# A Mamba block and a mixture of experts on one core: front stages further ahead, another order in each slot, all four scans in PSUM

## The chip, the cores and the metric

The kernel runs on one core of one Trainium2 chip. The metric is the device time of one execution in microseconds, as the median of several runs. All data are fp32.

## The reference

The input x has 8 sequences of 1024 tokens with 256 features. Cut to what matters:

```python
x = x + mamba(layernorm(x))            # mamba itself returns its input plus its output
x = x + moe(layernorm(x))

# mamba: d_inner 512, 16 states, conv of 4 taps, dt_rank 16
u, z = split(norm(x) @ W_in.T)
u = silu(causal_conv(u) + conv_b)
dt, B, C = split(u @ W_xp.T);  dt = softplus(dt @ W_dt.T + b_dt)
for t:  h = exp(dt[t] * A) * h + dt[t] * u[t] * B[t];  y[t] = sum_n(h * C[t])
out = (y + u * D) * silu(z) @ W_out.T

# moe: 8 experts, each token goes to its best 2
logits = x @ router_w + router_b;  w = softmax(top2(logits))
out[token] = sum over its two experts of w * (silu(x @ gate_e) * (x @ up_e)) @ down_e
```

## The kernel before, in words

The tokens are cut into 16 chunks q of 512 tokens, two to a sequence. The scan of a chunk is cut into 16 units (u = 16 q + n): unit n holds 4 of the 16 states for 128 of the 512 inner channels, spread as 4 tiles j of 128 partitions by 512 time steps. Two chunks make a group of 1024 tokens, whose MoE runs as 23 tiles of 128 sorted rows, each with the weights of one expert (768 KB, loaded anew for each tile).

Every engine runs the same loop over slots s (one scan unit each, then the slots of the tail), and in each slot its own part of several stages, in an order written out by hand. The engines are tied together by semaphores alone, and each executes its own instructions in order. A slot therefore has no fixed time; an engine can be a slot or two ahead of another as far as its waits allow.

- **The scan.** GpSimd (POOL) makes dt·u·B for the four tiles (`drive`, line 979, two instructions of 128x1024, one slot ahead, into one of three buffers `hs`). ScalarE (ACT) makes exp(dt·A) into the PSUM tile `dA` (`decay`, line 697). VectorE (DVE) scans tiles 0 and 1 in place in `dA` and multiplies both with C (`unit_first`, lines 778 and 789). In `unit_last` it scans tile 3 into `hs` in SBUF, then tile 2 in place, and multiplies tile 2 with C (line 800). GpSimd multiplies tile 3 with C (`weigh`, line 990). TensorE (PE) sums over the states into `yps` (its `weigh`, line 523).
- **The front and tail stages of a chunk** go through one PSUM bank `ring`, one item after the other: PE fills it, ACT (for O: DVE) empties it. The items are X0, X1 (transposes of the normalised input), U0 to U3 (projection to u), W0 to W3 (conv), P0 (projection to dt, B, C), D0 to D3 (dt projection, with the softplus after D1 and D3), Z0 to Z3 (projection to z), and for the chunk before O0, O1 (output projection), F0, F1 (transposes), R0 (router) and, for the second chunk of a group, K0 (ranks). `FRONT_RING` and `TAIL_RING` give the slot n of each. PE and ACT take the first item of a slot, then part of the MoE work, then the second item, then the rest.
- **Softplus.** ACT computes exp, 1+e and ln in `softplus`; DVE computes a rounding term (`round_off`, line 804); GpSimd adds it and multiplies with u (`dtu`, lines 996 to 1001, in slots 11 and 15). SP stores dt and dt·u to DRAM (`store_dt`, line 329) and loads them back spread over the partitions (`load_rep`, line 341).
- **Routing.** `route` (slot 5) adds the router bias on DVE (827), takes the top two and builds one-hot rows (827 to 841). `place` (slot 6) computes where each row goes, `scatter` (slots 7 to 14, GpSimd's indirect DMAs) sorts the rows into DRAM, `gather` (8 slots in a row after the last tile) brings two result rows per token back, and `combine` (one slot later, line 895) adds them.
- **MoE tiles.** Tile k passes through the slots at = k (transpose, line 542, eviction 712), k+1 (gate and up, 553, tanh 718), k+2 (`activate`, 885 and 888), k+3 (down, 534) and k+4 (store). SP's `load_tile` loads the sorted rows `xt` (353) and the gate and up weights (356) of tile at+1, after `store_tile` and `load_down` of the slot.

All plain DMAs are issued by SP, in one queue, in order; a wait on SP holds back every load behind it.

## Time and profile before

| | |
|---|---|
| median of 3 runs | 3042.28 us (3037.51 to 3044.11) |
| the profiled execution, its own time | 3046.68 us |
| its span in the profile | 3044.9 us |
| TensorE clock granted, mean | 0.817 of full |

The profile shows one execution. Its busy time per engine is a sum over stages that have different limits; the span runs from the first instruction to the last. Line numbers are those of the kernel before. In the rows a group of instructions is named line, engine, operation, output<-input; "idle before" is the idle time of that engine ahead of the group, and what ended it.

### The profile page before, as it was taken

The page shows a single profiled execution, that of the slowest core. Times are in us where ns is not written, and L with a number is a line of the kernel's source. Part 1 is how long each engine was busy: PE and PEld are TensorE (multiplying, and loading weights), DVE is VectorE, ACT ScalarE, POOL GpSimd, SP SyncE. Part 2 cuts the span into 40 slices and gives each one's busy share as a digit, 9 for nine tenths or more (in the row PEclk, how much of TensorE's full clock was granted, in tenths as well). Part 3 has the DMA queues.
Part 4 walks back from the last instruction along what each step waited for, and adds up shares of the span by engine and source line. Part 5 has one row for each costly group of instructions (what it writes and reads, how often), then busy time and mean ns, then how long its engine had stood idle before and what let it go on. Part 6 is the DMA issues. An engine that isn't in the chain of part 4 may idle for free.

```text
span 3044.9 us, 34043 instructions
## 1 busy us (share of the span) xinstructions
PE 1986.4 (65%) x8672; PEld 1105.0 (36%) x8672; DVE 2249.9 (74%) x3168; ACT 1533.8 (50%) x2414; POOL 2113.2 (69%) x1499
## 2 busy tenths in 40 slices
PE   4465665786747685586846867487764868556564
PEld 1112131444315351254414443154522535144453
DVE  0498988887868688787877878687887878789322
ACT  2565746465544655456454565446544564534111
POOL 0697869767696678867697676967688666976312
PEclk9687877798868897798867988688977989668888
DMA  3533343667457764566637574567736766375576
GB/s 122 141 91 96 95 114 84 179 169 187 110 158 184 183 185 113 163 185 177 159 112 197 155 202 116 149 177 189 190 99 169 191 163 173 110 200 158 163 213 193
DMA packets 271490, 473.01 MB, mean 155 GB/s; under 512 B 36928, under 2 KB 114752, under 8 KB 271168
## 3 DMA queue, kind: packets, MB, share of 16 engines
q1 hardware_dynamic: 259008, 437.26, 53.6%
q0 software_dynamic: 12288, 33.57, 3.5%
q8 instruction: 72, 1.18, 0.2%
q14 instruction: 122, 1.00, 0.1%
HBM read 372.38 MB, written 98.30 MB: 155 GB/s over the span
## 4 chain that ended last, share of the span: by engine, by line
POOL 32%; issue 17%; DVE 15%; PE 14%; DMA 9%; SPq 6%; ACT 6%; POOLq 0%; DVEq 0%; ACTq 0%
POOL hs L979 16%; DMA xt<-sorted_x 6%; DVE dA L778 5%; POOL sorted_x L1007 4%; PE p_g L553 4%; DVE hs L778 3%; POOL hs L990 3%; POOL pair L1017 2%; POOL dtb L998 2%; POOL dtub L996 2%; PE ring L443 2%; PE ring L435 2%; SPq L341 2%; DMA out<-xr 1%; PE p_a L534 1%
## 5 line engine op out<-in xcount | busy, mean ns | idle before, releaser
L979 POOL TENSOR_TENSOR hs<-rep_dtu,b_bc 128x1024 f32<-128x1024 f32 x512 | 1195.8, 2360 | 24.1 <-DMA rep_dtu<-dt_d 14.3
L697 ACT ACTIVATE dA<-rep_dt,a_s 128x512 f32<-128x512 f32 x1024 | 675.8, 684 | 616.3 <-DVE hs L789 453.7
L523 PE MATMUL yps<-hs,const_s 128*32 128x512 f32 x2048 | 335.0, 730 | 361.6 <-POOL hs L990 327.0
L990 POOL TENSOR_TENSOR hs<-hs,c_bc 128x512 f32<-128x512 f32 x256 | 330.5, 1291 | 343.9 <-DVE hs L778 333.0
L778 DVE TENSOR_TENSOR_SCAN dA<-dA,hs 128x512 f32<-128x512 f32 x384 | 453.5, 1211 | 56.1 <-POOL hs L979 46.7
L778 DVE TENSOR_TENSOR_SCAN dA<-dA,carry,hs 128x512 f32<-128x512 f32 x384 | 476.6, 1272 | 14.8 <-POOL hs L979 11.7
L553 PE MATMUL p_g<-xy,w_e 128*128 128x128 f32 x2944 | 424.1, 306 | 41.5 <-DVE hT L888 41.4
L553 PEld LDWEIGHTS p_g<-xy,w_e 128*128 128x128 f32 x2944 | 414.7, 223 | 75.2 <-issue 72.3
L435 PE MATMUL ring<-xnT,w_in_s 128*128 128x512 f32 x512 | 329.8, 778 | 104.3 <-ACT sz L634 64.3
L789 DVE TENSOR_TENSOR hs<-dA,c_bc 128x1024 f32<-128x1024 f32 x256 | 312.1, 1219 | 4.4
L885 DVE SCALAR_TENSOR_TENSOR th<-th,p_g 128x256 f32<-128x256 f32 x184 | 76.5, 416 | 312.1 <-ACT th L718 312.0
L712 ACT ACTIVATE xy<-p_a 128x512 f32<-128x512 f32 (+1 forms) x208 | 113.3, 545 | 326.4 <-PE p_a L542 298.2
L443 PE MATMUL ring<-ubuf,d_conv 128*128 128x512 f32 x512 | 249.1, 631 | 4.7 <-ACT ubuf L625 3.3
L542 PE MATMUL p_a<-const_s,xt 128*128 128x128 f32 x368 | 87.4, 325 | 246.1 <-DMA xt<-sorted_x 220.9
L895 DVE SCALAR_TENSOR_TENSOR xr<-pair,w,xr 128x256 f32<-128x256 f32 x64 | 73.7, 1151 | 219.2 <-DMA pair<-sorted_y,pos 210.1
L523 PEld LDWEIGHTS yps<-hs,const_s 128*32 128x32 f32 x2048 | 46.2, 117 | 513.9 <-issue 458.7
L1017 POOL DMA_INDIRECT pair<-sorted_y,pos x128 | 125.1, 977 | 152.7 <-DMA sorted_y<-xy 90.7
L435 PEld LDWEIGHTS ring<-xnT,w_in_s 128*128 128x128 f32 x512 | 109.7, 238 | 283.9 <-issue 143.1
L534 PE MATMUL p_a<-w_e,hT 128*128 128x256 f32 x736 | 209.7, 411 | 1.1 <-DVE hT L888 1.1
L800 DVE TENSOR_TENSOR hs<-dA,c_bc 128x512 f32<-128x512 f32 x256 | 175.6, 686 | 4.4
L534 PEld LDWEIGHTS p_a<-w_e,hT 128*128 128x128 f32 x736 | 142.1, 204 | 70.1 <-issue 49.0
L1007 POOL DMA_INDIRECT sorted_x<-xf,pos x128 | 129.3, 1010 | 52.7 <-issue 50.8
(113 smaller groups left out, 2805.1 us busy)
## 6 DMA issues: line engine op xcount, KB each, us to landing
w_e<-in_w_moe SPq DMA_DIRECT2D x184, 512.0 KB
rep_dt<-dt_d SPq DMA_DIRECT2D x256, 256.0 KB
rep_dtu<-dt_d SPq DMA_DIRECT2D x256, 256.0 KB, 8.7
w_e<-in_w_moe SPq DMA_DIRECT2D x184, 256.0 KB
xt<-sorted_x SPq DMA_DIRECT2D x184, 128.0 KB
sorted_y<-xy SPq DMA_DIRECT2D x184, 128.0 KB
dt_d<-dtb SPq DMA_DIRECT2D x32, 512.0 KB
dt_d<-dtub SPq DMA_DIRECT2D x32, 512.0 KB
```

The costliest lines, as they stand in the source:

```text
L435: last = pe.matmul(ring[:], w_in_s[:, c, ch * P:(ch + 1) * P], xnT[:, c, :], start=c == 0, stop=c == DC - 1)
L443: last = pe.matmul(ring[:], d_conv[:, c, k, :], ubuf[:, c % 2, k:k + T], start=k == 0, stop=k == TAPS - 1)
L523: last = pe.matmul(yps[32 * j:32 * j + 32, :], sumsel, hs[:, u % 3, j, :], start=False, stop=g == G - 1, skip_group_check=True)
L534: last = pe.matmul(p_a[:, DM:2 * DM], hT[:, v % 2, c, :], w_e[:, v % 2, col:col + DM], start=c == 0, stop=c == DC - 1)
L553: last = pe.matmul(p_g[:, f, :], w_e[:, v % 2, col:col + P], xtT(v)[:, c, :], start=c == 0, stop=c == DC - 1)
L697: act.activation(dA[:, j, :], rep_dt[:, c % 2, j, :], ACT.Exp, scale=a_s[:, n, j:j + 1]).then_inc(s_exp, 1)
L778: return dve.tensor_tensor_scan(out_ap, dA[:, j, :], hs[:, u % 3, j, :], init, ALU.mult, ALU.add)
L789: dve.tensor_tensor(hs[:, u % 3, 0:2], dA[:, 0:2], c_bc[:, g, :].unsqueeze(1).to_broadcast([P, 2, T]), ALU.mult).then_inc(s_m01, 1)
L979: pool.tensor_tensor(hs[:, u % 3, a:a + 2], rep_dtu[:, c % 2, a:a + 2], b_bc[:, g, :].unsqueeze(1).to_broadcast([P, 2, T]), ALU.mult).then ...
L990: pool.tensor_tensor(hs[:, u % 3, 3], hs[:, u % 3, 3], c_bc[:, g, :], ALU.mult).then_inc(s_hp, 1)
L1007: pool.indirect_dma_start(out=sorted_x[g.b], out_offset=bass.IndirectOffsetOnAxis(ap=pos[:, g.b, k, i:i + 1], axis=0), in_=xf[:, (g.first ...
L1017: pool.indirect_dma_start(out=pair[:, v % 2, k, :], out_offset=None, in_=sorted_y[g.b], in_offset=bass.IndirectOffsetOnAxis(ap=pos[:, g.b, ...
```

## The change

- `FIRST` moves from -19 to -23, and every front item of a chunk is placed by its distance to the chunk's first unit (`PLACES`): X0, X1, U0 at -19, three slots earlier than before, P0 at -10 (before: -7), D0 and D1 at -9 (-6), D2 and D3 at -5 (-2), Z2 and Z3 at -4. O, F and R keep their slots, K0 comes one slot later.
- In each slot PE now does its `weigh`, then the MoE tile (down, transpose, gate and up), and then all ring items. ACT does two decays, `take_pa`, `tanh`, the other two decays, and then all ring items. DVE does `round_off`, `route`, `place`, `weights` and `combine` between `unit_first` and `unit_last`, where they came after `unit_last`.
- GpSimd's work on dt is split: `smooth` (two instructions) in slots 8 and 12, `dtu` (one) in slots 9 and 13. Its `weigh` is gone.
- All four scans write in place to `dA`; DVE multiplies tiles 2 and 3 with C in one instruction of 128x1024.
- SP: the sorted rows of tile at+1 are loaded first in a slot, before everything else, and its gate and up weights last. `store_dt` is in slots 10 and 14, `store_bc` in 7.
- The router's bias is added by one more matmul on PE; the one-hot rows are made by one DVE instruction in place of a copy and eight comparisons.
- Scatter starts one slot later; for all groups but the last the gathers are two slots apart; `combine` follows two slots after its gather.

```diff
-FIRST = -UN - 3
-SCATTER = 7
+FIRST = -UN - 7
+SCATTER = 8
...
-        self.gather = self.start + STAGES + 1
+        step = 2 if per == 1 else 1
+        self.gather = {k: self.start + STAGES + 1 + step * k for k in range(NT)}
...
-FRONT_RING = {0: ["X0", "X1", "U0"], 3: ["W0"], 4: ["U1"], 5: ["W1"], 6: ["U2", "U3"], 7: ["W2"], 8: ["W3"], 9: ["P0"],
-              10: ["D0", "D1"], 11: ["Z0", "Z1"], 12: ["Z2"], 13: ["Z3"], 14: ["D2", "D3"]}
-TAIL_RING = {1: ["O0"], 2: ["O1"], 4: ["F0", "F1"], 5: ["R0"], 6: ["K0"]}
+PLACES = {-19: ["X0", "X1", "U0"], -18: ["U1"], -17: ["W0"], -16: ["W1"], -13: ["U2", "U3"], -12: ["W2"], -11: ["W3"],
+          -10: ["P0"], -9: ["D0", "D1"], -8: ["Z0"], -6: ["Z1"], -5: ["D2", "D3"], -4: ["Z2", "Z3"],
+          17: ["O0"], 18: ["O1"], 20: ["F0", "F1"], 21: ["R0"], 23: ["K0"]}
+SMOOTH = {8: 0, 12: 1}
...
SP:
-            for s in range(-UN, TOTAL_SLOTS):
+            for s in range(FIRST, TOTAL_SLOTS):
                 q, n = s // UN, s % UN
                 front = 0 <= q + 1 < NQ
+                for g, at in moe_at(s):
+                    if 0 <= at + 1 < NK:
+                        load_tile(g, at + 1)
+                    if 0 <= at - 4 < NK:
+                        store_tile(g, at - 4)
+                for g, i in gathered(s - 3):
+                    store_out(g, i)
+                for g, i in gathered(s - 1):
+                    load_xr(g, i)
...
                 for g, at in moe_at(s):
-                    if 0 <= at - 4 < NK:
-                        store_tile(g, at - 4)
                     if 0 <= at - 1 < NK:
                         load_down(g, at - 1)
                     if 0 <= at + 1 < NK:
-                        load_tile(g, at + 1)
+                        load_expert(g, at + 1)
...
PE:
-                items = ring_in(s)
-                for item in items[:1]:
-                    through_ring(item)
                 for g, at in moe_at(s):
                     if 0 <= at - 3 < NK:
                         down(g, at - 3)
                     if 0 <= at < NK:
                         tile_transpose(g, at)
-                for item in items[1:2]:
-                    through_ring(item)
-                for g, at in moe_at(s):
                     if 0 <= at - 1 < NK:
                         gate_up(g, at - 1)
-                for item in items[2:]:
+                for item in ring_in(s):
                     through_ring(item)
...
ACT:
                 if scan:
-                    for j in (0, 1, 3):
+                    for j in (0, 1):
                         decay(s + 1, j)
...
                 for g, at in moe_at(s):
                     if 0 <= at < STAGES:
                         take_pa(g, at)
-                if scan:
-                    decay(s + 1, 2)
-                for item in items[1:2]:
-                    through_ring(item)
-                for g, at in moe_at(s):
                     if 0 <= at - 1 < NK:
                         tanh(g, at - 1)
-                for item in items[2:]:
+                if scan:
+                    for j in (2, 3):
+                        decay(s + 1, j)
+                for item in ring_in(s):
                     through_ring(item)
-                if n == 15 and 0 <= q + 2 < NQ:
+                if n == 12 and 0 <= q + 2 < NQ:
                     norm_x(q + 2)
...
DVE:
-                scan(u, 3).then_inc(s_h3, 1)
-                scan(u, 2).then_inc(s_scan, 1)
+                scan(u, 2)
+                scan(u, 3).then_inc(s_scan, 1)
                 dve.wait_ge(s_scan, 2 * u + 2)
                 if q % 2 == 0:
-                    dve.tensor_copy(carry[:, n, 2:3], dA[:, 2, T - 1:T]).then_inc(s_carry, 1)
-                dve.tensor_tensor(hs[:, u % 3, 2], dA[:, 2], c_bc[:, g, :], ALU.mult).then_inc(s_m2, 1)
+                    dve.tensor_copy(carry[:, n, 2:4], dA[:, 2:4, T - 1]).then_inc(s_carry, 1)
+                dve.tensor_tensor(hs[:, u % 3, 2:4], dA[:, 2:4], c_bc[:, g, :].unsqueeze(1).to_broadcast([P, 2, T]),
+                                  ALU.mult).then_inc(s_m2, 1)
...
+                if n in SMOOTH and 0 <= q + 1 < NQ:
+                    round_off(2 * (q + 1) + SMOOTH[n])
+                if tail and n == 6:
+                    route(q - 1)
...
POOL:
-                if 0 <= s < UN * NQ:
-                    weigh(s)
-                if n in (11, 15) and 0 <= q + 1 < NQ:
-                    dtu(q + 1, int(n == 15))
+                if n in SMOOTH and 0 <= q + 1 < NQ:
+                    smooth(q + 1, SMOOTH[n])
+                if n - 1 in SMOOTH and 0 <= q + 1 < NQ:
+                    dtu(q + 1, SMOOTH[n - 1])
```

## Rows read from the trace of the kernel before

**Rows 1.** Windows: us, PE, PEld, DVE, ACT, POOL busy, clock, DMA share, GB/s.

```profile
114.90:377.70 262.80, 160.37 (x500) 53.16 (x504) 235.09 (x286) 165.27 (x242) 232.56 (x152) 0.80 0.44 104
377.70:711.00 333.30, 228.26 (x932) 117.71 (x924) 268.27 (x365) 185.02 (x286) 247.54 (x170) 0.79 0.53 141
...
1424.60:1782.30 357.70, 245.90 (x1088) 139.56 (x1084) 280.68 (x397) 190.47 (x300) 263.76 (x186) 0.81 0.60 162
...
2497.10:2822.00 324.90, 210.69 (x996) 125.00 (x988) 279.84 (x378) 148.47 (x241) 245.68 (x159) 0.80 0.59 160
2822.00:3044.90 222.90, 119.28 (x748) 102.83 (x748) 51.95 (x145) 34.44 (x75) 48.17 (x53) 0.82 0.63 190
```

**Rows 2.** Windows: about slots 9 to 16 of the period from 1424.6.

```profile
1516.10:1618.60 102.50, 52.51 (x143) 16.70 (x141) 72.07 (x92) 58.92 (x82) 93.98 (x76) 0.65 0.42 120
```

**Rows 3.** Groups by form, whole run: busy us, mean ns | idle before.

```profile
L990 POOL TENSOR_TENSOR hs<-hs,c_bc 128x512 f32<-128x512 f32 x256 | 330.5, 1291 | 343.9 <-DVE hs L778 333.0
L789 DVE TENSOR_TENSOR hs<-dA,c_bc 128x1024 f32<-128x1024 f32 x256 | 312.1, 1219 | 4.4
L800 DVE TENSOR_TENSOR hs<-dA,c_bc 128x512 f32<-128x512 f32 x256 | 175.6, 686 | 4.4
L778 DVE TENSOR_TENSOR_SCAN dA<-dA,carry,hs 128x512 f32<-128x512 f32 x384 | 476.6, 1272 | 14.8 <-POOL hs L979 11.7 <-ACT dA L697 3.0
L778 DVE TENSOR_TENSOR_SCAN hs<-dA,carry,hs 128x512 f32<-128x512 f32 x128 | 163.3, 1276 | 0.0
L443 PE MATMUL ring<-ubuf,d_conv 128*128 128x512 f32 x512 | 249.1, 631 | 4.7 <-ACT ubuf L625 3.3 <-ACT uc L629 0.8 <-ACT lgr L680 0.6
```

**Rows 4.** Waits of the period 1424.6 to 1782.3: total us, times, longest.

```profile
DVE th L885 <- ACT th L718: 34.5, 11, 11.3
...
DVE xr L895 <- DMA pair<-sorted_y,pos: 28.3, 6, 9.3
PE p_a L542 <- DMA xt<-sorted_x: 28.0, 5, 9.7
```

**Rows 5.** Waits of SP's queue, whole run.

```profile
SPq L329 <- POOL dtub L1001: 328.5, 28, 28.4
```

**Rows 6.** Timeline of SP, 1748 to 1762: start us, us.

```profile
1749.93 0.35 SPq L356 DMA_DIRECT2D w_e<-in_w_moe  x1
...
1759.47 0.43 SPq L353 DMA_DIRECT2D xt<-sorted_x  x1
```

**Rows 7.** Timeline of PE behind it.

```profile
1767.30 0.69 PE L542 MATMUL p_a<-const_s,xt 128*128 128x128 f32 x2 [9.70 <-DMA xt<-sorted_x]
```

**Rows 8.** Timeline of DVE in `route`.

```profile
1485.07 0.75 DVE L827 TENSOR_TENSOR lg<-lgr,rb_s 128x32 f32<-128x32 f32 x1 [1.29 <-ACT lgr L680]
...
1486.26 1.84 DVE L832 TENSOR_TENSOR gap<-mx 128x4 f32<-128x4 f32 x1
...
1488.90 1.16 DVE L839 TENSOR_SCALAR hot<-const_s,ixf 128x8 f32<-128x8 f32 x8
1490.09 0.19 DVE L841 TENSOR_TENSOR hot<-hot 128x32 f32<-128x32 f32 x1
```

**Rows 9.** Timeline of POOL beside it.

```profile
1483.42 4.65 POOL L979 TENSOR_TENSOR hs<-rep_dtu,b_bc 128x1024 f32<-128x1024 f32 x2
```

**Rows 10.** Timeline of ACT, dt and softplus of one half chunk.

```profile
1772.12 1.06 ACT L653 ACTIVATE ubuf<-xn_t 128x1024 f32<-128x1024 f32 x1
1773.19 1.28 ACT L655 ACT_TABLE_LOAD   x1
```

**Rows 11.** Timeline of ACT around the first decays.

```profile
114.13 2.52 ACT L697 ACTIVATE dA<-rep_dt,a_s 128x512 f32<-128x512 f32 x4
116.59 2.06 ACT L597 ACTIVATE xn_t<-xs,rst 128x256 f32<-128x256 f32 x4
```

**Rows 12.** Windows of the last group's tiles, with and without gathers beside them.

```profile
2884.00:2925.00 41.00, 19.26 (x96) 16.77 (x97) 9.12 (x20) 4.47 (x10) 14.02 (x16) 0.70 0.64 192
2925.00:3008.00 83.00, 58.98 (x389) 50.41 (x387) 16.60 (x39) 17.07 (x36) 0.46 (x1) 0.94 0.79 238
```

More of the change, by code:

```diff
@@ L727, in _ @@
                     norm_x2(q - 1)
-                items = ring_in(s)
-                for item in items[:1]:
-                    through_ring(item)
                 for g, at in moe_at(s):
@@ L907, in _ @@
                         activate(g, at - 2)
+                if n in SMOOTH and 0 <= q + 1 < NQ:
+                    round_off(2 * (q + 1) + SMOOTH[n])
+                if tail and n == 6:
+                    route(q - 1)
+                for g in ALL:
+                    if s == g.scatter[0]:
+                        place(g)
+                    if s == g.scatter[0] + 1:
+                        weights(g)
+                for g, i in gathered(s - 2):
+                    combine(g, i)
                 if unit:
                     unit_last(s)
-                if n in (11, 15) and 0 <= q + 1 < NQ:
-                    round_off(2 * (q + 1) + (n == 15))
                 if unit and n in (4, 8, 12):
@@ L919, in _ @@
                     moments(1, q - 1)
-                if tail and n == 5:
-                    route(q - 1)
-                for g in ALL:
-                    if s == g.scatter[0] - 1:
-                        place(g)
-                    if s == g.scatter[0] + 1:
-                        weights(g)
-                if n == 13 and 0 <= q + 2 < NQ:
+                if n == 10 and 0 <= q + 2 < NQ:
                     moments(0, q + 2)
-                for g, i in gathered(s - 1):
-                    combine(g, i)
         @block.gpsimd
```

83 lines of the change are left out of this document (27 added, 56 removed).

## The prediction

> **What bounds the kernel now.** I read first the windows between the first scans of the chunks. They show a steady pattern: the first scan at 114.9 us, a first group of two chunks without MoE in 262.8 us, one of 333.3, then five periods of 32 slots like that from 1424.6, which takes 357.7 us, a last one of 324.9, and 222.9 us after the last scan [rows 1]. In the steady period DVE is busy 280.7 us and so idle 77; POOL is busy 263.8, PE 245.9, ACT 190.5. No engine is full. Each slot ends when DVE has scanned, so what counts is DVE's work plus the time in which DVE stands still.
>
> The idle time comes from three places. In slots 9 to 16 POOL is busy 94.0 of 102.5 us and DVE only 72.1: scatter, the three dt instructions and its own C product meet on POOL [rows 2]. This is 30 of the 77 us. Second, the waits of the period name what came late: `activate` waits 34.5 us for the tanh, which waits for PE, and PE's tile transpose waits 28.0 us for the sorted rows, `combine` 28.3 us for the gathered pair [rows 4]. Third, what is behind the late rows is SP: it stands 328.5 us in all before `store_dt` for POOL's last dt instruction, up to 28 us at once [rows 5]. The example at 1750: SP issues the expert weights of one tile at 1749.93, then reloads dt, B and C, and only at 1759.47 the sorted rows of the next tile [rows 6]. PE stands 9.7 us and gets them at 1767.30 [rows 7].
>
> **DVE's work after.** The second C product grows from 128x512 to 128x1024, from 686 to 1219 ns, so by 0.53 us in each unit [rows 3]: 17.1 us in a period of 32, 136 in all. No scan is added; the fourth moves its output from SBUF to PSUM, 1276 against 1272 ns [rows 3], which I take as nothing. In `route` the bias add (0.75 us), the copy and the eight comparisons (1.16 us) fall away [rows 8], and one comparison comes. It reads two SBUF tensors, and such an instruction is bounded by two rows: 0.19 us for the sum of the one-hot rows, 1.84 us for a 4-element subtraction that starts while POOL runs `drive` and ends at 1488.10, just when POOL does, at 1488.07 [rows 8, 9]. So `route` gains between 0.2 and 1.9 us; I take 1.5, because with its C product gone POOL is freer: 3 us a period. DVE's work in the steady period is 280.7 + 17.1 - 3 = 294.8 us.
>
> **POOL's work after.** 1.29 us per unit and a small copy go [rows 3], 41 us a period and more. Better, POOL no longer waits for DVE's third scan inside its slot; `drive` is held only by the three `hs` buffers, so POOL can be up to two slots ahead. In slots 9 to 16 its work falls from 94 to about 81 us, its dt work is in two pieces, and three to four of the gathers come there instead of all eight. DVE's own 72 us [rows 2] grow there by 8 times 0.53 and some waiting. POOL should no longer set these slots; I count that idle time as gone, but for what the dt chain itself costs (below). If POOL still set them, up to 9 us a period would come back (81 against 72).
>
> **SP.** The sorted rows are issued right behind the weights of the tile before: in the example at about 1750.4 in place of 1759.5, nine us earlier, and the PE wait of 9.7 us is covered [rows 6, 7]. `store_dt` is asked for one slot after POOL's `dtu` instead of in the slot right behind it. What is queued behind it on SP are B, C and the expert weights, which have two slots until they are used. With gathers two slots apart `store_out` is issued two slots before the load that reuses its buffer, and the pair has two slots to land. I take the waits for sorted rows and pairs in the periods as gone. The bytes are the same.
>
> **What becomes late next.** ACT now empties the first ring item of a slot only behind the last two decays, and those wait for DVE's product at the end of its slot. In a slot with several items PE is stuck at the second one until DVE has ended the slot, and PE's next `weigh` and MoE tile come behind it. I walked through one chunk with the durations of the trace (a conv item is eight matmuls of 0.63 us that overlap, 3.7 us from first to last; an unloaded slot of DVE is about 8.1 us):
> - Slot 4 (F0, F1, W2): the second item starts about 3 us into DVE's slot 5, the conv ends at 8, ACT's next decay is ready at 9.5. DVE waits 1.5 to 2 us; with slot 5 (R0, W3 and the silu with two table loads) some 5 us in all.
> - Slot 7 (D0, D1) and `round_off` in slot 8: dt's two evictions, exp and 1+e end only 5 us after the middle of DVE's slot, since 1.06 us instructions stand in a row there with no slack [rows 10], and `round_off` is now in the middle of the slot, with two scans behind it: 5 us.
> - Slot 11 (D2, D3) and `round_off` in slot 12: 3 us, as there is no MoE work in every other of these.
> - Slot 12 (Z2, Z3, silu, then eight normalisation instructions, 4.1 us by twice the 2.06 [rows 11]): 5 us. Slot 13 (X0, X1, U0): 1.5 us.
>
> This is 19.5 us a chunk, 39 a period. The bound below is none at all, if ACT and PE catch up in the slots between; the bound above is the 77 us of now, as if every stall only moved.
>
> **The sum.** Steady period 294.8 + 39 = 334, so 24 less, five times: -120. The second group, 268.3 busy of 333.3 [rows 1]: + 14 + 36 = 318, -15. The last, 279.8 of 324.9, with no front stages in its second half: 318, -7. The first, 235.1 of 262.8: + 14 gives 249, and without MoE half of the stalls, 20: 269, +6. The start: X0, X1, U0 and U1 of chunk 1, its normalisation and Z2, Z3 now stand in ACT's order ahead of the first decay at 114.13; before, the normalisation followed it at 116.59 [rows 11]. 4 us of normalisation, about 12 for four items through the ring and 6 for Z2, Z3 and their silu: +22, an estimate from the durations above. The tail: while gathers run beside the tiles, PE is busy 19.3 of 41 us and the cores' DMA share is 0.64; later it is busy 59.0 of 83 at 0.79 [rows 12]. With `load_xr` no longer behind its own buffer's store and the sorted rows early I take 12 us off the first and 8 off the second: -20. In all -134. The profiled execution took 3046.7 us, 4.4 more than the median of the runs, so 2912.7 less 4.4: 2908 us.
>
> **Rivals.**
> - *DVE bound, stalls small.* The walk may be too strict, as ACT and PE have 167 and 112 us to spare in a period [rows 1]. With 15 us idle in the steady period it takes 310, -48 five times, with the other stretches in proportion -310 in all: about 2730. For it: of the 77 us idle now, 34.5 and 28.3 already have the names tanh and pair [rows 4], so the ring's evictions themselves cost DVE little. Against: all of these had the first item ahead of the waiting decay.
> - *The convoy.* Each slot with several ring items holds PE until DVE has ended, and the MoE tile and the tanh behind it hold ACT's last decays, so the delay goes round instead of being caught up. It decides from 63 us idle in a steady period on (357.7 - 294.8), 31 a chunk instead of my 19.5. With 77, as now, a period costs 372: +14 five times, the start +22, the first group +14, the others +25, the tail -20, about 3150. For it: seven of 16 slots have two or three items. Against: the idle time of now has named causes, most of which the change takes away.
> - *The lock between POOL and DVE.* The rows show a DVE instruction with two SBUF inputs waiting for the end of POOL's [rows 8, 9]. `combine`, `route`, `place` and `round_off` move to the middle of the slot, where POOL, now early, runs `drive` (4.65 us of some 9). Some 17 such instructions a period (eight in `combine`, the rest in `route`, `place`, `weights` and `round_off`) at up to 2.3 us, half of one 4.65, would be 39 us. Part of it is paid already, as the 1.84 shows; if 24 of it are new, the steady gain is gone and the time is about 3040, no change. The Trainium skill states the same rule in SBUF — State Buffer, Who interferes with whom: whichever of the two starts first keeps the shared ports for its whole instruction. By that rule the new product of C costs nothing extra, having one input in PSUM; that agrees with L789's 1219 ns, twice 686 less a fixed part.
>
> **The fourth scan by the page.** The Trainium skill says in ScalarE: Activation LUTs, Step-by-step: what each stage is for, that VectorE is placed closer to SBUF. By it the fourth scan would take longer in PSUM than before, and the sum would rise by an amount that the page doesn't give; the two rows of scans, 1272 in PSUM and 1276 into SBUF, show no such cost [rows 3].
>
> **Chances and range.** Forecast, stalls between 20 and 55 us a period: 0.64. Small stalls: 0.22. Convoy: 0.07. Lock or another cost that eats the gain, within a few us of now or above: 0.07. A run of this kernel can tell 0.2% from no change, 6 us. Faster 0.90, same 0.02, slower 0.08. The range takes the forecast's own, 2810 to 2990, and reaches down to where most of the small-stall case lies: 2760 to 2990.
>
> **What would show it.** Right: a steady period of 325 to 345 us with DVE busy 290 to 300 in it; no wait of PE for sorted rows and of DVE for pairs worth naming; SP's wait for POOL's dtu below 100 us; DVE's idle time at slots 4 to 8 and 12 to 14, named by exp or ubuf; the first scan near 137 us; the C products of 128x1024 at 1219 ns, 512 of them. Wrong: POOL still busy over 90% in slots 9 to 16; DVE's two-SBUF instructions longer than now; a first scan at 115; PE idle waiting for ACT's ring evictions in every slot.

## The result: 5.8% slower, and the profile after

The changed kernel takes 3218.4 us (median of 4 runs, 3217.1 to 3218.9) beside 3042.8 us before (4 runs): 1.058 times, 95% interval 1.0562 to 1.0598. The forecast of 2908 us was wrong in sign, and the time lies outside the range. The profiled execution has a span of 3217.0 us.

Windows of the changed kernel, cut at the first scans of the groups as in [rows 1]: first group, second, one steady period of 32 slots, last, and all behind the last scan.

```profile
130.70:431.50 300.80, 175.03 (x502) 56.28 (x500) 247.25 (x277) 164.84 (x242) 179.10 (x100) 0.74 0.37 89
431.50:777.30 345.80, 225.40 (x899) 111.25 (x900) 272.96 (x346) 180.28 (x280) 203.68 (x123) 0.79 0.48 128
1534.70:1913.60 378.90, 258.32 (x1090) 138.33 (x1090) 311.47 (x380) 188.06 (x299) 220.21 (x139) 0.80 0.56 153
2673.60:3011.70 338.10, 216.35 (x989) 122.38 (x988) 299.82 (x360) 141.38 (x229) 191.40 (x108) 0.78 0.55 152
3011.70:3217.00 205.30, 117.95 (x772) 100.81 (x772) 51.69 (x138) 35.32 (x77) 47.98 (x52) 0.84 0.67 211
```

The edges are as forecast: the end behind the last scan takes 205 us (203 expected, 223 before), and the first scan comes at 130.7 us (137 expected, 114.9 before). Timeline of ACT there, answering to [rows 11]:

```profile
113.98 2.06 ACT L590 ACTIVATE xn_t<-xs,rst 128x256 f32<-128x256 f32 x4
...
129.95 2.52 ACT L690 ACTIVATE dA<-rep_dt,a_s 128x512 f32<-128x512 f32 x4
```

The normalisation and the ring items of the next chunk now stand ahead of the first decay. Everything between is longer. In the steady period DVE is busy 311.5 us where I had 294.8, and idle 67.4 where I had 39.

Groups by form of the changed kernel, whole run (busy us, mean ns | idle before), answering to [rows 3]:

```profile
L763 DVE TENSOR_TENSOR_SCAN dA<-dA,carry,hs 128x512 f32<-128x512 f32 x512 | 629.2, 1274 | 134.2 <-ACT dA L690 134.2
L763 DVE TENSOR_TENSOR_SCAN dA<-dA,hs 128x512 f32<-128x512 f32 x512 | 598.2, 1214 | 132.6 <-ACT dA L690 130.7 <-issue 1.4
L785 DVE TENSOR_TENSOR hs<-dA,c_bc 128x1024 f32<-128x1024 f32 x256 | 312.3, 1220 | 4.4
L878 DVE SCALAR_TENSOR_TENSOR xr<-pair,w,xr 128x256 f32<-128x256 f32 x64 | 98.6, 1541 | 2.3
L876 DVE SCALAR_TENSOR_TENSOR xr<-pair,w,xr 128x256 f32<-128x256 f32 x64 | 98.1, 1534 | 60.2 <-DMA xr<-x_d 38.4 <-DMA pair<-sorted_y,pos 21.8
L834 DVE TENSOR_SCALAR w<-gap 128x8 f32<-128x8 f32 x8 | 16.7, 2082 | 0.0
L858 DVE CAST pos<-posf 128x16 uint32<-128x16 f32 x8 | 14.2, 1781 | 0.3
```

The fourth scan costs nothing in PSUM (1274 ns), and the product of C takes 1220 ns. What is new is at the end of the scans' lines and in the last four lines: the scans stood 264.9 us for ACT's decays (25.0 of it once, ahead of the first scan), where they had stood 11.9 us before, 3.0 of it in the group that [rows 3] shows; and `combine`'s instructions take 1.54 us each, where they took 1.15 and 0.53.

The waits of DVE, whole run (total us, times, longest):

```profile
DVE dA L763 <- ACT dA L690: 265.0, 55, 25.0
DVE ubuf L790 <- ACT ubuf L646: 224.0, 32, 67.9
DVE xs L801 <- PE ring L458: 89.2, 24, 6.0
DVE th L866 <- ACT th L711: 73.2, 33, 5.8
```

The pair and the tanh, the two names that headed DVE's waits in [rows 4], have shrunk: 21.8 us for the pair, and of the 73.2 us for the tanh 72.1 lie behind the last scan. In their place stand three others, all behind the ring: decays, dt (`ubuf`) and the output projection (`xs`). Of the wait for dt 87.2 us lie ahead of the first scan, where the kernel before had 93.2; the other 136.8 are new. The output projection had 20.3 us before. On SP the wait of [rows 5] has gone down too: over the two lines of `store_dt` it was 328.5 and 59.6 us before and is 68.5 and 54.6 now, 123.1 together, where the prediction wanted less than 100.

Now the same steady period in eight windows of four slots each, a chunk in four rows:

```profile
1534.70:1576.90 42.20, 34.23 (x171) 23.59 (x171) 35.14 (x53) 15.32 (x26) 18.85 (x12) 0.91 0.63 165
1576.90:1622.90 46.00, 41.06 (x195) 23.31 (x194) 33.85 (x58) 24.83 (x42) 22.01 (x10) 0.90 0.56 152
1622.90:1670.10 47.20, 21.34 (x61) 6.09 (x61) 41.19 (x59) 20.66 (x31) 28.58 (x26) 0.73 0.47 117
1670.10:1721.80 51.70, 26.17 (x68) 8.38 (x68) 43.24 (x39) 31.28 (x46) 42.90 (x28) 0.69 0.35 101
1721.80:1769.80 48.00, 32.63 (x138) 20.78 (x138) 42.68 (x45) 13.97 (x25) 26.75 (x18) 0.75 0.61 164
1769.80:1817.70 47.90, 37.54 (x178) 21.10 (x178) 38.60 (x54) 24.82 (x43) 25.48 (x14) 0.93 0.69 196
1817.70:1865.00 47.30, 31.02 (x134) 16.72 (x134) 42.93 (x47) 23.07 (x35) 28.62 (x23) 0.78 0.60 164
1865.00:1913.60 48.60, 34.34 (x149) 18.36 (x150) 33.83 (x36) 34.12 (x51) 27.04 (x13) 0.75 0.63 172
```

Length less DVE's busy time is its idle time. Averaged over the two chunks it is 6.2 us in slots 0 to 3, 10.7 in 4 to 7, 5.2 in 8 to 11 and 11.6 in 12 to 15. The walk of the prediction had 0, 5, 5 and 9.5. The waits bear out the names: in slots 0 to 3 DVE waits 6.5 and 4.8 us for the output projection, in 4 to 7 10.1 and 7.4 for decays, in 8 to 11 5.3 and 3.8 for dt. So the dt and Z stalls were sized nearly right, the conv stall at half, and the one of the output projection was not seen at all.

The new wait can be followed in one place of the period: PE and ACT are in slot 4 with their ring items, DVE in slot 5 and about to begin slot 6. First DVE, then ACT, then PE, each a timeline of the changed kernel (start us, us, in brackets the idle time before it).

```profile
1587.86 1.21 DVE L774 TENSOR_TENSOR hs<-dA,c_bc 128x1024 f32<-128x1024 f32 x1
...
1592.23 1.22 DVE L785 TENSOR_TENSOR hs<-dA,c_bc 128x1024 f32<-128x1024 f32 x1
1599.28 2.35 DVE L763 TENSOR_TENSOR_SCAN dA<-dA,hs 128x512 f32<-128x512 f32 x2 [5.84 <-ACT dA L690]
```

```profile
1587.94 1.29 ACT L690 ACTIVATE dA<-rep_dt,a_s 128x512 f32<-128x512 f32 x2
1589.17 0.58 ACT L670 ACTIVATE xn_t<-ring 128x512 f32<-128x512 f32 x1
1591.01 0.60 ACT L670 ACTIVATE xn_t<-ring 128x512 f32<-128x512 f32 x1 [1.26 <-PE ring L465]
1597.84 0.69 ACT L622 ACTIVATE uc<-ring,chan_s 128x512 f32<-128x512 f32 x1 [6.23 <-PE ring L441]
1598.56 1.30 ACT L690 ACTIVATE dA<-rep_dt,a_s 128x512 f32<-128x512 f32 x2
```

```profile
1589.80 1.11 PE L465 MATMUL ring<-const_s,xf 128*128 128x128 f32 x4 [1.73 <-ACT xn_t L670]
1591.66 6.09 PE L441 MATMUL ring<-ubuf,d_conv 128*128 128x512 f32 x8 [0.75 <-ACT xn_t L670]
```

Read it from below. The slot has three ring items: two F transposes (`L465`) and a conv (`L441`). All three stand behind the tile on PE, and their evictions behind ACT's last two decays at 1587.94. The ring has one buffer, so each item waits for the eviction of the one before. The conv starts at 1591.66 and takes 6.09 us; ACT stands 6.23 us for it. The next two decays write tiles 0 and 1, which are free since DVE's product at 1587.86 ended at 1589.07, but they stand behind all three evictions and start at 1598.56. DVE, done with its slot at 1593.45, scans at 1599.28, after 5.84 us idle.

### The profile page after: what moved, and what is told of

Read it like the earlier page. It is cut to its first block and busy times, and to the rows that moved or that the text cites. A ratio compares the mean times of both kernels' runs of the same rounds, so it can differ in the third digit from the quotient of the medians.

```text
span 3217.0 us, 33179 instructions
## 1 busy us (share of the span) xinstructions
PE 2084.9 (65%) x8704; PEld 1100.8 (34%) x8704; DVE 2434.7 (76%) x3024; ACT 1516.2 (47%) x2414; POOL 1759.2 (55%) x1115
## 3 DMA queue, kind: packets, MB, share of 16 engines
q0 software_dynamic: 12288, 33.57, 3.2%
## 5 line engine op out<-in xcount | busy, mean ns | idle before, releaser
L763 DVE TENSOR_TENSOR_SCAN dA<-dA,carry,hs 128x512 f32<-128x512 f32 x512 | 629.2, 1274 | 134.2 <-ACT dA L690 134.2
L763 DVE TENSOR_TENSOR_SCAN dA<-dA,hs 128x512 f32<-128x512 f32 x512 | 598.2, 1214 | 132.6 <-ACT dA L690 130.7
L552 PEld LDWEIGHTS p_g<-xy,w_e 128*128 128x128 f32 x2944 | 398.4, 217 | 156.5 <-issue 155.4
L785 DVE TENSOR_TENSOR hs<-dA,c_bc 128x1024 f32<-128x1024 f32 x256 | 312.3, 1220 | 4.4
L774 DVE TENSOR_TENSOR hs<-dA,c_bc 128x1024 f32<-128x1024 f32 x256 | 312.2, 1220 | 4.4
L441 PE MATMUL ring<-ubuf,d_conv 128*128 128x512 f32 x512 | 281.5, 701 | 27.1 <-ACT ubuf L618 8.3
L967 POOL TENSOR_TENSOR dtub<-dtub,ubuf 128x1024 f32<-128x1024 f32 x32 | 75.5, 2359 | 329.6 <-ACT dtub L648 323.4
L790 DVE SCALAR_TENSOR_TENSOR ubuf<-ubuf,xn_t 128x1024 f32<-128x1024 f32 x32 | 57.0, 1782 | 224.0 <-ACT ubuf L646 224.0
L452 PE MATMUL ring<-xd,w_dt_s 128*128 128x512 f32 x128 | 111.8, 970 | 173.5 <-ACT dtb L639 159.3
L711 ACT ACTIVATE th<-p_g 128x256 f32<-128x256 f32 x184 | 69.8, 380 | 221.1 <-PE p_g L552 219.2
L441 PEld LDWEIGHTS ring<-ubuf,d_conv 128*128 128x128 f32 x512 | 109.1, 224 | 170.3 <-issue 126.8
```

Of the source, the lines that this page charges most:

```text
L441: last = pe.matmul(ring[:], d_conv[:, c, k, :], ubuf[:, c % 2, k:k + T], start=k == 0, stop=k == TAPS - 1)
L452: pe.matmul(ring[:], w_dt_s[:, c * P:(c + 1) * P], xd[:], start=True, stop=True).then_inc(s_ring, 1)
L552: last = pe.matmul(p_g[:, f, :], w_e[:, v % 2, col:col + P], xtT(v)[:, c, :], start=c == 0, stop=c == DC - 1)
L763: return dve.tensor_tensor_scan(dA[:, j, :], dA[:, j, :], hs[:, u % 3, j, :], init, ALU.mult, ALU.add)
L774: dve.tensor_tensor(hs[:, u % 3, 0:2], dA[:, 0:2], c_bc[:, g, :].unsqueeze(1).to_broadcast([P, 2, T]), ALU.mult).then_inc(s_m01, 1)
L785: dve.tensor_tensor(hs[:, u % 3, 2:4], dA[:, 2:4], c_bc[:, g, :].unsqueeze(1).to_broadcast([P, 2, T]), ALU.mult).then_inc(s_m2, 1)
```

## The experiments

All ratios are against runs of the kernel before on the same chip, with 95% intervals; those runs had medians of 3034.6 to 3042.8 us, so a difference between kernels of two comparisons is sure to some 8 us. "Period" is a steady period of 32 slots cut at first scans. Two theories for the loss stood at the start: *ring order* (the items behind the tile on PE, and behind the tile and the last decays on ACT) and *lock* (DVE's two-input instructions moved beside POOL's `drive`).

**1. Only `combine` back at the end of the slot.**

```diff
-                for g, i in gathered(s - 2):
-                    combine(g, i)
                 if unit:
                     unit_last(s)
...
+                for g, i in gathered(s - 2):
+                    combine(g, i)
```

> The changed kernel with combine moved back behind unit_last, nothing else. Lock theory: in the middle of the slot combine's two instructions wait for POOL's drive (2.01 and 1.85 us each in a steady period against 1.34 and 0.48 before), so with the move the second falls to about 0.5 us, DVE's busy time in a steady period falls from 311 us to about 296 and the kernel is some 15 us a period, about 80 to 110 us, faster than the changed one: near 3120. Rival, the ring theory: the stalls set the slots and DVE's longer instructions fill time in which it would have waited anyway; then under 20 us come back, 3200 or more.

Measured: 3129.3 us, 1.0305 (1.0269 to 1.0342), 89 us less than the changed kernel's 3218.4 (93 by the spans, 3217.0 and 3123.8). The groups by form of this kernel:

```profile
L876 DVE SCALAR_TENSOR_TENSOR xr<-pair,w,xr 128x256 f32<-128x256 f32 x64 | 66.6, 1040 | 62.0 <-DMA xr<-x_d 39.1 <-DMA pair<-sorted_y,pos 22.9
L878 DVE SCALAR_TENSOR_TENSOR xr<-pair,w,xr 128x256 f32<-128x256 f32 x64 | 41.0, 641 | 2.3
```

The two instructions fall from 98.1 + 98.6 to 66.6 + 41.0 us, 89 less, which is the whole gain as nearly as it can be told. And the period, 16.5 us shorter, is so by busy time, with hardly any idle time gone (66.1 idle against 67.4):

```profile
1502.70:1865.10 362.40, 253.49 (x1093) 137.25 (x1092) 296.31 (x380) 187.96 (x299) 220.29 (x139) 0.82 0.58 160
```

So the lock is real: `combine` in the middle of the slot costs 15 us a period, 89 in all. It does not explain a loss of 310 against the forecast alone.

**2. Only the ring order of before, on PE and ACT**, all else as changed:

```diff
+                items = ring_in(s)
+                for item in items[:1]:
+                    through_ring(item)
                 for g, at in moe_at(s):
...
+                for item in items[1:2]:
+                    through_ring(item)
...
-                for item in ring_in(s):
+                for item in items[2:]:
                     through_ring(item)
```

> The changed kernel with the old order of ring items on PE and ACT: first item ahead of the MoE tile and ahead of the two decays that wait for DVE's last product, the second between, the rest behind. Ring theory: the stalls in slots 1, 2, 5, 6, 8, 12, 13 and 14 come from evictions that stand behind those decays, so DVE's idle time in a steady period falls from 67 us to about 35 and in the first group, which has no MoE, from 53 to about 25; time near 3000. Rival: the stalls come from where the items were placed (D right before round_off, the normalisation behind Z3) and not from the order in a slot; then the idle time stays above 55 us a period and the time above 3150.

Measured: 3034.1 us, 0.9988 (0.9972 to 1.0004): 184 us less than the changed kernel, within the bound of the time before. Windows of a period and of the first group:

```profile
1450.60:1804.00 353.40, 250.44 (x1089) 142.67 (x1088) 299.82 (x379) 189.21 (x300) 221.16 (x139) 0.83 0.60 165
131.20:411.10 279.90, 176.20 (x503) 56.41 (x501) 250.67 (x277) 166.23 (x244) 178.98 (x100) 0.76 0.39 93
```

Idle time falls from 67 to 54 us in the period and from 54 to 29 in the first group. The period is 25.5 us shorter, and only 14 of this is idle time: DVE's busy time falls too, by 12 us, and `combine`'s two instructions from 30.9 to 18.9 us in it, though they stay in the middle of the slot. So 184 us is the price of the ring order together with most of the lock that comes with it. Its waits:

```profile
DVE th L878 <- ACT th L717: 279.5, 81, 9.5
DVE ubuf L802 <- ACT ubuf L652: 122.5, 20, 67.6
DVE dA L775 <- ACT dA L696: 83.6, 27, 25.9
```

The decays fall from 265.0 to 83.6 us, dt from 224.0 to 122.5 (86.9 of it ahead of the first scan), but the tanh is back, 73.2 to 279.5. Items ahead of the tile make the tile late; items behind it make the next decays late. In this kernel the second is dearer.

**3. The kernel before with SP's order and the gathers two slots apart.** The move that I had counted on, alone, with `combine` left at the slot's end:

```diff
+                for g, at in moe_at(s):
+                    if 0 <= at + 1 < NK:
+                        load_tile(g, at + 1)
...
-        self.gather = self.start + STAGES + 1
+        self.gather = {k: self.start + STAGES + 1 + step * k for k in range(NT)}
```

> The kernel before with two parts of the change: the sorted rows first in SP's slot with the expert weights last, and the gathers two slots apart with combine two slots behind (at the end of the slot, as before). If the waits for sorted rows (28 us a period on PE) and for pairs (28 us on DVE) were on the path, the period falls from 357.7 to about 325 and the time to about 2850. Rival: POOL, which is full in slots 9 to 16, and its dt work behind SP's wait set those stretches anyway; then DVE's wait for the pair turns into a wait for POOL's drive and the time is 3000 to 3040.

Measured: 2892.0 us, 0.952 (0.9491 to 0.9549), a gain of 145 us.

**4. The kernel before with all scans in PSUM and all C products on DVE.**

```diff
-                dve.tensor_tensor(hs[:, u % 3, 2], dA[:, 2], c_bc[:, g, :], ALU.mult).then_inc(s_m2, 1)
+                dve.tensor_tensor(hs[:, u % 3, 2:4], dA[:, 2:4], c_bc[:, g, :].unsqueeze(1).to_broadcast([P, 2, T]),
+                                  ALU.mult).then_inc(s_m2, 1)
...
-            def weigh(u):
```

> The kernel before with one part of the change: all four scans in PSUM and all products of C on DVE. Two sizes are told apart. If DVE sets the slots, the 0.53 us per unit are paid in full, 136 us, near 3180. If POOL's load is what sets slots 9 to 16 and its product at the slot's end holds PE back, its 1.3 us per unit saved outweigh that there and the time lies between 2980 and 3060. The forecast of the prediction, with POOL's relief counted as larger than DVE's burden, wants the second.

Measured: 2968.3 us, 0.9769 (0.9739 to 0.9798), a gain of 68 us although DVE's work grew by 20 us a period, to 300.8 of 344.7. Its idle time fell from 77 to 44. POOL, relieved of 43 us (220.5 against 263.8), had been one of the causes of DVE's waits, as the prediction had read from [rows 2]. The edit also moves ACT's decay of tile 3 behind the first ring item and `take_pa`, next to that of tile 2, since tile 3 is now free only with it.

**5. Both, on the kernel before** (the edits of 3 and 4 together).

> The kernel before with the two parts that gained alone: sorted rows first and gathers apart (2892 us, -145), and four scans in PSUM with all C products on DVE (2968 us, -68). If their gains are of different kinds (SP's queue, POOL's load) they add: near 2825. Rival: both relieve the same stretch, slots 9 to 16, where in the first DVE still waited 150 us in all for POOL's drive; then the second gains there more than alone, or, if DVE is now full, its 136 us of extra work eat the rest and it is 2870 to 2900. DVE's busy time in a steady period should be about 300 us, so 2780 is a floor.

Measured: 2806.4 us, 0.9251 (0.9232 to 0.9271). The gain of 230 us is a little more than the sum of the two, 213: each removes a wait that the other does not. In 3 alone DVE still waits 150.1 us for POOL's `drive`, in 4 alone 115.5 us for the pair; here it is 77.1 and 22.7.

**6. And the router's bias by a matmul with one comparison.**

```diff
-                then(dve.tensor_tensor(lg[:], lgr[:].rearrange("p (i e) -> p i e", e=NE),
-                                       rb_s[:].unsqueeze(1).to_broadcast([P, QT, NE]), ALU.add))
...
-                for i in range(QT):
-                    for k in range(2):
-                        last = dve.tensor_scalar(hot[:, k, at + i, :], iota, ixf[:, i, k:k + 1], None, ALU.is_equal)
+                then(dve.tensor_tensor(hot[:, 0:2, at:at + QT], ...
```

> As the run with rows first, gathers apart and C products on DVE, and the router's bias as a matmul and one comparison in place of a copy and eight. At most 1.9 us of DVE's work per chunk go, 30 us in all; if DVE's chain in slot 5 is the path, 20 to 30 us less than that run; if slot 5 waits for ACT's eviction of R0 anyway, under 10.

Measured: 2792.1 us, 0.9203 (0.9184 to 0.9222), the fastest kernel of the study. These are the changes that the prediction counted as gains (but for the split of POOL's dt work), without the new placement and without the new order in the slot. Its period, and the waits in it (its first group takes 267.3 us):

```profile
1333.10:1654.90 321.80, 235.92 (x1092) 136.80 (x1088) 292.49 (x379) 189.14 (x300) 220.62 (x138) 0.85 0.65 180
```

```profile
DVE th L884 <- ACT th L723: 12.8, 4, 5.2
DVE dA L781 <- POOL hs L978: 9.9, 5, 4.0
```

DVE is busy 292.5 us, near the 294.8 of the prediction, and idle 29.3.

**7. The changed kernel with all of DVE's side work behind the last product** (`round_off`, `route`, `place`, `weights` and `combine`).

```diff
                 if unit:
                     unit_last(s)
+                if n in SMOOTH and 0 <= q + 1 < NQ:
+                    round_off(2 * (q + 1) + SMOOTH[n])
+                if tail and n == 6:
+                    route(q - 1)
...
```

> The changed kernel with all of DVE's side work (round_off, route, place, weights, combine) back behind unit_last, as before; ring order as changed. Against the run with combine alone moved (3129 us, stalls of 4.7 us in each of slots 8 and 12 of a chunk without MoE) this tells what round_off in the middle of the slot costs. Theory: at the end of the slot ACT has 3.5 us more, so the two stalls shrink from about 4.5 to 1 to 2 us each, 32 of them, and the time is 3040 to 3090. Rival: ACT's softplus holds its own next decays back as well, so the stall only moves to the scan behind it, and the time stays within 15 us of 3129.

Measured: 3089.1 us, 1.0183 (1.0149 to 1.0217), 40 us less than experiment 1. In the period (355.1 us, busy 301.15) DVE is idle 54.0 us in place of the 66.1 of experiment 1. In the middle of the slot `round_off` waits for dt with two scans behind it that could have run; at the end it waits less, 114.7 us over the run in place of 196.9, since they are done by then. Against this DVE is busy 5 us a period more, for `combine` takes 132.3 us over the run here and 107.6 in 1.

**8. Ring order of before and side work at the end** (the edits of 2 and 7).

> The changed kernel with the old order of ring items and all of DVE's side work back at the end of the slot: what stays of the change are the placement of the front stages, the split dt work, the C products, the router and SP's order. If the orders inside the slots are all that went wrong, this lies well below the kernel before, at 2850 to 2950. Rival: the placement itself is bad (several items with softplus or silu in slots 8, 12 and 13); then the stalls seen in slots 6, 8, 12 and 24 of the run with ring order alone (3034 us, 300 us busy and 53 idle a period) stay, and only combine's 16 us a period come back: 2930 to 2960.

Measured: 2942.6 us, 0.9693 (0.9671 to 0.9715). The gains overlap in part: 184 and 129 alone, 276 together. This kernel has all of the change but for its order in the slot, and it is faster than before by 94 us. It lies near to the forecast's 2908, but in part by luck, since two errors cancel in part: DVE is idle 34 us a period, 5 less than forecast, and busy 307.6, 13 more.

**9. On ACT alone, ring items ahead of the last two decays.** A theory of mine on the mechanism of 2: that ACT's order is what counts.

```diff
+                for item in ring_in(s):
+                    through_ring(item)
                 if scan:
                     for j in (2, 3):
                         decay(s + 1, j)
-                for item in ring_in(s):
-                    through_ring(item)
```

> The changed kernel with one swap on ACT alone: the ring items of a slot come ahead of the last two decays instead of behind them; PE and DVE as changed. The theory says that evictions stand behind decays that wait for the end of DVE's slot. Then this swap alone frees PE early: DVE's wait for exp (265 us in all) and for PE's output projection (89 us) shrink, and the time falls by 80 to 180 us, to 3040 to 3140. Rival: what counts is that PE does its ring items behind the MoE tile, so ACT could not evict them much earlier anyway, and the decays now stand behind PE's items; then DVE's wait for exp grows and the time stays at 3200 or rises.

Measured: 3185.4 us, 1.0499 (1.0478 to 1.052), only 33 us less. DVE's wait for dt (`ubuf`) goes from 224.0 to 144.8 us, but that for the decays from 265.0 to 395.9, 131 more: the items still start behind the tile on PE, and now this slot's decays stand behind their evictions. DVE's idle time even grows, from 67 to 74 us a period; what makes the run shorter is its busy time, 297.9 in place of 311.5 us, as `combine` falls from 196.7 to 142.8 us over the run. My theory fell. The order on PE has to change with it, as in 2; a likely reason is that the first item is then on its way while ACT does the early decays, but the order on PE alone was not tried.

**10. The kernel of 6 with POOL's dt work split over two slots**, as in the change, and its store one slot later (and the first reload with it).

```diff
-                    dtu(q + 1, int(n == 15))
+                    smooth(q + 1, int(n == 15))
+                if n == 12 and 0 <= q + 1 < NQ:
+                    dtu(q + 1, 0)
+                if n == 0 and 0 <= q < NQ:
+                    dtu(q, 1)
```

> The best kernel so far (2792 us: the one before, with rows first, gathers apart, C products on DVE and the router's shorter route) with the dt work of POOL split as in the change: two instructions in slots 11 and 15, the third behind the next slot's drive, and SP's store one slot later. DVE still waits 73 us for drive there. If splitting helps by itself, 10 to 30 us less; if the later store makes SP hold the sorted rows and weights back, or the reload of dt comes late for the next chunk, 0 to 30 us more. It also says what of the 150 us between this kernel and the changed one with both orders undone (2943 us) belongs to the split and not to the placement of the front stages.

Measured: 2853.5 us, 0.9399 (0.9381 to 0.9418), 61 us slower than 6. With dt made as late as in the kernel before, the store and the reload come a slot later, and POOL waits for the reload before `drive`, 164.8 us over the run in place of 15.6. DVE's longest wait for `drive` grew from 4.3 to 12.5 us, its sum only from 73.4 to 90.2. Of the 62 us by the spans 34 are idle time of DVE and 28 busy time; `combine` takes 142.0 us in place of 94.0. So the lateness of dt is one part of the price and the lock the other; they were not separated.

**11. The kernel of 8 with the dt work in one piece.** The control for 10 in the changed placement.

```diff
                     smooth(q + 1, SMOOTH[n])
-                if n - 1 in SMOOTH and 0 <= q + 1 < NQ:
-                    dtu(q + 1, SMOOTH[n - 1])
+                    dtu(q + 1, SMOOTH[n])
```

> The changed kernel with both orders undone (2943 us) and the three dt instructions of POOL again in one piece, in slots 8 and 12. In the kernel before, splitting them cost 61 us, because drive came between and the store came later. If the split costs here as well, this run is 10 to 40 us below 2943. If the front stages, three slots ahead, give the dt chain room enough, splitting or not makes no difference (2930 to 2960), and what is left of the 150 us to the best kernel belongs to the placement. If POOL in one piece holds drive back next to the scatters, which now overlap it, 10 to 40 us more.

(The 61 us named there were measured on the kernel of 6, in 10.)

Measured: 2949.5 us, 0.9705 (0.9676 to 0.9735), not distinguishable from 8. With the front stages as early as there the split costs nothing and gives nothing. The parts do move: in a period DVE is busy 301.5 us and idle 38.6 where 8 has 307.6 and 33.9. So busy time that goes does not always shorten the run; it can come back as waiting.

**12. The kernel of 8 with P0 behind the tile**, the item that falls into slot 6 (of a chunk in work) beside the backlog of slots 4 and 5.

```diff
                 items = ring_in(s)
+                if items and items[0][1] == "P0":
+                    items = [None, None] + items
```

> The changed kernel with both orders undone (2943 us), but in the one slot of a chunk whose first ring item is P0, that item comes behind the MoE tile on PE and ACT. In that run DVE idles 9.1 and 7.8 us in slots 6 of the two chunks of a period, waiting for the tanh: P0 needs the silu behind W3 of the slot before, and stands ahead of the MoE tile on PE. If that is the cause, both fall below 3 us and the time to 2840 to 2880. Rival: the stall is the backlog of slots 4 and 5 (F0, F1, W2, R0, W3) and comes whatever P0 does; then 2920 to 2950.

Measured: 2939.0 us, 0.9673 (0.9641 to 0.9705), no different from 8, and DVE's wait for the tanh in the period has the same longest time, 9.2 us. That P0 itself delays the tile is refuted. What is left is the backlog of five items in slots 4 and 5 (F0, F1, W2, R0, W3). The windows of 8 show its place: in slots 4 to 7 DVE is idle 11.1 us (44.70 less 33.57), in the slots before it 0.6.

```profile
1408.80:1444.30 35.50, 32.10 (x175) 21.91 (x174) 34.95 (x52) 16.34 (x29) 17.87 (x12) 0.96 0.81 224
1444.30:1489.00 44.70, 39.79 (x209) 25.12 (x207) 33.57 (x57) 24.21 (x40) 22.02 (x10) 0.92 0.57 153
```

I didn't try to spread these five items, so this part is argued and not shown.

## Why the prediction was wrong

**What held.** The end of most waits for pairs (DVE's wait for pairs 210.1 to 21.8 us over the run), the price of the C product, the free fourth scan, the relief of POOL, the later first scan, the shorter end. Experiments 3 to 6 show that these parts alone are worth 244 us (3036.5, the time before in that comparison, less 2792.1), because without the new order and placement DVE's idle time goes down to 29 us a period and not to 39.

**The step that failed first: "What becomes late next".** The stalls are 67 us a period and not 39. Term by term (per chunk, forecast against measured): output projection 0 against 6.2, conv 5 against 10.7, dt in slot 8 5 against 5.2, slots 12 to 15 9.5 against 11.6. The mechanism was named rightly, an item that starts behind the tile and a decay that stands behind its eviction; two terms of the walk were wrong. It left out O0 and O1, whose product DVE itself takes out of the ring: DVE waited 89.2 us in 24 places for it, 3.7 us each, for a PE that has the tile first. And it put slots 4 and 5 at 5 us. In the place shown above, counted from the start of DVE's slot 5 at 1585.42, the walk had the second item at 3 us, the end of the conv at 8 and the decays ready at 9.5; measured are 4.4, 12.3 and 13.9. The items start 1 to 2 us later than in the walk, and the conv takes 6.09 us and not 3.7. This was no exception: the conv of slot 4 took 5.4 to 6.4 us in all 14 chunks in which the F transposes stand ahead of it. DVE waited 5.84 us there and 4.23 a slot later, 10.1 in all. Experiment 2 puts the price of the ring order, with the part of the lock that goes with it, at 184 us; with the side work already at the slot's end (7 against 8) it is 147.

**The step "without MoE half of the stalls" failed too.** The first group has 53.5 us idle (300.80 less 247.25) and not 20. No tile stands in the way there, but the items start behind the last decays all the same. In the first group the changed kernel is 21 us longer than with the ring order of before (300.8 against 279.9). ACT's two late decays wait for DVE's product at the end of its slot, with or without MoE.

**The lock was put too low.** As a rival it decided the sign at 24 us a period; it was new by 15 (311.5 busy against 296.3 in experiment 1). I gave it 0.07 and zero in the sum, though the row with 1.84 us for a 4-element subtraction was before me [rows 8, 9]. It should have been a term of its own. Its bound of 2.3 us for one instruction was too low: ten instructions of `combine` took 5.3 to 7.0 us each, and one 7.5. That it held single-input instructions too was not in the prediction (both below).

**Together.** The steady period is 378.9 against 334: 28 us of it idle and 17 busy, five times, 225 in all; the first group +32, the second +28, the last +20, the start −6, the end +2. That is 301 of the 304 us between the 2912.7 of the sum and the span of 3217.0.

**The convoy rival** came nearest: it gave about 3150 and decided from 63 us idle a period on; there were 67.4. I held against it that the idle time of before had causes which the change removes. It does remove them, as 3 to 6 show, but that does not limit the new waits, which are made by the new order and have nothing to do with the old ones.

**What stays open.** The loss against 8 (276 us) is the orders inside the slot, since 8 differs from the changed kernel in nothing else. The 150 us between 8 (2942.6) and 6 (2792.1) belong to what still differs between these two: the placement of the front stages further ahead, with the normalisation, the routing, the scatter and the stores of dt, B and C that moved with it (the split of dt is ruled out by 11). In part it is seen: the first scan at 133.7 in place of 114.7; the first group 277.7 in place of 267.3; and in the period DVE busy 307.6 in place of 292.5:

```profile
1408.80:1750.30 341.50, 249.73 (x1091) 140.09 (x1090) 307.57 (x380) 189.09 (x300) 220.61 (x139) 0.84 0.62 170
```

The 15 us of busy time are nearly all in `combine`: in 8 its two instructions take 115.6 + 50.8 us, in 6 they take 51.1 + 42.9, and 12 of them are over 3 us in 8, none in 6. The slot's end is no safe place in itself; it depends on where POOL is. But by experiment 11 less busy time there need not give less time in all, so how much of the 150 us it costs isn't shown, nor which stage's place costs the rest.

## What to carry to other kernels

In an order written out by hand, with one buffer between two engines, ask of each item that you move back not only who uses its result but what is queued behind its eviction on the second engine: here the next slot's decays, which hold the bounding engine. Walk through all slots with all their items, those that the bounding engine takes out itself too, and with durations from a place that has waits like those to come; a walk with the shortest duration of the conv, and without two of the items, gave 39 of 67 us. Moving small instructions of DVE beside a long one of POOL is a cost to put in the sum, not among the rivals, and where a change has parts with separate reasons, run them apart: the good parts were worth −244 us here, inside a change that measured +176.

## What the runs showed of the hardware

**DVE instructions with one small SBUF input were held by POOL too.** `w<-gap` (`L834`, a constant operation on 128x8) took 2082 ns on average where it took 818 before and 244 in experiment 6; the cast of 128x16 took 1781 ns. A timeline of the changed kernel, DVE and beside it POOL:

```profile
889.76 2.03 DVE L834 TENSOR_SCALAR w<-gap 128x8 f32<-128x8 f32 x1
891.82 0.20 DVE L835 RECIPROCAL w<-w 128x8 f32<-128x8 f32 x1
...
889.39 2.35 POOL L975 TENSOR_TENSOR dtub<-dtb,uc 128x1024 f32<-128x1024 f32 x1
```

Both end within 0.05 us of each other, 891.79 and 891.74. The reciprocal behind it, of the same size, takes 0.20, but no such product of POOL runs beside it. The products with an input in PSUM were 1220 ns throughout. The Trainium skill has the rule in SBUF — State Buffer, Who interferes with whom: casts and constant operations can enter a mode that takes both ports, and then block; instructions with one SBUF input outside that mode do not. The trace agrees for casts, constant operations and the products, with the numbers above.

**One DVE instruction was held by several of POOL in a row.** The changed kernel, DVE and beside it POOL:

```profile
1690.78 6.98 DVE L876 SCALAR_TENSOR_TENSOR xr<-pair,w,xr 128x256 f32<-128x256 f32 x1
...
1690.50 4.67 POOL L960 TENSOR_TENSOR hs<-rep_dtu,b_bc 128x1024 f32<-128x1024 f32 x2
1695.12 2.34 POOL L975 TENSOR_TENSOR dtub<-dtb,uc 128x1024 f32<-128x1024 f32 x1
```

POOL's three products run without a gap from 1690.50 to 1697.46, and `combine`'s first instruction, which took 0.47 us where it was fastest, ends 0.30 us behind the last, at 1697.76. This came once in each steady period. So a product of POOL that starts while DVE is already waiting went ahead of it here.

**The same conv took 3.70 and 6.09 us within 15 us.** Windows of the changed kernel ahead of and in the first (`L441` at 1591.66), and around the second (at 1605.17):

```profile
1580.00:1589.70 9.70, 6.80 (x39) 4.04 (x38) 9.56 (x14) 7.31 (x15) 4.90 (x3) 1.00 1.05 243
1589.70:1596.50 6.80, 5.95 (x10) 2.88 (x11) 3.71 (x5) 0.65 (x2) 0.00 (x0) 0.50 0.82 268
1605.00:1609.00 4.00, 3.83 (x12) 1.59 (x16) 3.51 (x17) 0.16 (x2) 0.00 (x0) 1.00 0.33 121
```

The granted clock was 1.00, all at the upper of its two levels (2.4 GHz), until 1589.7, then 0.50, all at the lower one (1.2 GHz), and 1.00 again around the second conv. Before it fell, PE had just stood 1.73 us for ACT's eviction; the wait of 0.75 us came after. The conv of slot 4 met this in each of its 14 chunks (5.4 to 6.4 us); the one of slot 5, ahead of which PE stood 0.29 us, took 3.70 us in eight of them and 5.40 in six. So a slower clock belongs to this place in the order, and it makes ACT and DVE wait longer, but that the waits in the ring bring it about isn't shown. Nor does the mean clock of a period follow DVE's idle time: it is 0.80 in the changed kernel with 67 us idle, but 0.84 with 74 in experiment 9, as in 8 with 34. How much of the 276 us runs through the clock was not separated.
